# VectorE: addresses and wait values ahead of the drains, and a step's group sums ahead of the strong add of the expert before

## The reference, cut to what matters

```python
for l in range(L):                                   # L = 3
    agg = jax.ops.segment_sum(h[src], dst, num_segments=N) / deg
    logits = jnp.concatenate([h, agg], axis=-1) @ router_W[l] + router_b[l]
    vals, idx = jax.lax.top_k(logits, TOPK)
    gates = jax.nn.softmax(vals, axis=-1)
    gate_dense = jnp.zeros_like(logits).at[rows, idx].set(gates)
    weak = jax.nn.relu(jnp.einsum('nh,ehf->nef', agg, weak_W[l]) + weak_b[l])
    sh = jax.nn.relu(jnp.einsum('nh,ehf->nef', agg, strong_W1[l]) + strong_b1[l])
    strong = jnp.einsum('nef,efh->neh', sh, strong_W2[l]) + strong_b2[l]
    moe = jnp.einsum('ne,neh->nh', gate_dense, jnp.concatenate([weak, strong], axis=1))
    conf = jax.nn.sigmoid(h @ conf_W[l] + conf_b[l])
    h = h + conf * moe
```

## Time and profile before

| What | us |
|---|---|
| Median of 3 runs | 8162.51 |
| The profiled execution | 8152.95 |
| Its span in the profile | 8151.3 |
| Preparation, to the first transposes of means | 567 |
| Expert loops of layers 0, 1, 2, last two steps included | 1461, 1468, 1413 |

### The profile page before, as it was taken

One profiled execution on the slowest core, in us unless ns is written; L12 is line 12 of the kernel. 1 busy time (PEld: TensorE's weight loads), 2 busy tenths in 40 slices (PEclk: granted clock), 3 DMA queues, 4 the chain that ended last, 5 costly groups with the idle time before them and its releaser, 6 DMA issues.

```text
span 8151.3 us, 58255 instructions
## 1 busy us (share of the span) xinstructions
PE 3661.2 (45%) x12045; PEld 2192.1 (27%) x12045; DVE 3263.1 (40%) x6294; ACT 1297.7 (16%) x2725; POOL 4118.8 (51%) x4324
## 2 busy tenths in 40 slices
PE   3137777776577777674866757760000000000000
PEld 2124444443444433344433434450000000000000
DVE  2124444443243433333433333433445444454553
ACT  0002222222122212221222222221000000000000
POOL 5664445444454444444444353426556565665565
PEclk6558888887688888786887878875555555555555
DMA  2342222222322222223212121212122122111111
GB/s 67 86 113 70 66 70 76 73 73 69 85 74 64 65 72 67 72 71 90 61 56 67 54 70 54 58 32 49 44 48 47 45 48 41 45 46 44 41 45 42
DMA packets 259372, 500.85 MB, mean 61 GB/s; under 512 B 104429, under 2 KB 146344, under 8 KB 258878
## 3 DMA queue, kind: packets, MB, share of 16 engines
q0 software_dynamic: 176592, 446.04, 21.0%
q1 hardware_dynamic: 62718, 36.97, 1.7%
q10 hardware_dynamic: 19952, 16.60, 0.6%
HBM read 464.44 MB, written 34.88 MB: 61 GB/s over the span
## 4 chain that ended last, share of the span: by engine, by line
PE 34%; issue 24%; another core or an unknown queue 16%; DVEq 12%; DVE 8%; ACT 2%; POOL 2%; ACTq 1%; DMA 0%; SPq 0%; POOLq 0%
PE ps_w1a L1949 6%; PE ps_w1b L1949 6%; PE ps_gate L1974 5%; PE ps_wide L1974 4%; PE ps_weak_a L1961 3%; PE ps_weak_b L1961 3%; DVE ps_wide L1395 2%; DVEq L1427 2%; DVEq L1367 1%; DVEq L1440 1%; PE ps_weak_a L1933 1%; POOL ring L660 1%; DVEq L1437 1%; DVEq L1420 1%
## 5 line engine op out<-in xcount | busy, mean ns | idle before, releaser
L660 POOL DMA_INDIRECT ring<-hidden_tab,stage x2400 | 2290.5, 954 | 2632.1 <-DVE ps_wide L974 1675.1
L660 POOL DMA_INDIRECT ring<-gat_tab,stage x1600 | 1527.7, 955 | 1186.1 <-issue 664.8
L1949 PE MATMUL ps_w1a<-agg_team_t,wbuf 128*128 128x512 f32 (+1 forms) x1248 | 661.9, 649 | 324.3 <-issue 163.6
L1949 PE MATMUL ps_w1b<-agg_team_t,wbuf 128*128 128x512 f32 (+1 forms) x1248 | 626.1, 627 | 127.4 <-ACT strong L1603 81.0
L1974 PE MATMUL ps_gate<-wbuf,strong 128*128 128x256 f32 x2400 | 607.2, 394 | 108.0 <-issue 107.3
L980 DVE TENSOR_TENSOR ps_wide<-ps_wide,ring 128x1024 f32<-128x1024 f32 x418 | 515.7, 1234 | 229.8 <-issue 229.6
L1147 DVE TENSOR_TENSOR h_res<-h_res,x_res 128x1024 f32 (+2 forms) x117 | 136.2, 1164 | 1104.5 <-ACT x_res L1612 1059.4
L1974 PE MATMUL ps_wide<-wbuf,strong 128*128 128x256 f32 x2304 | 571.7, 397 | 0.9 <-issue 0.9
L2088 PE MATMUL ps_w1a<-ident,agg_team_t 128*128 128x128 f32 x28 | 7.8, 434 | 1255.8 <-DVE agg_team_t L1473 1114.5
L1974 PEld LDWEIGHTS ps_gate<-wbuf,strong 128*128 128x128 f32 x2400 | 448.8, 197 | 245.2 <-issue 180.9
L1974 PEld LDWEIGHTS ps_wide<-wbuf,strong 128*128 128x128 f32 x2304 | 440.3, 202 | 89.7 <-issue 7.4
(11 more groups left out here) (406 smaller groups left out, 4725.0 us busy)
## 6 DMA issues: line engine op xcount, KB each, us to landing
ring<-hidden_tab,stage POOLq DMA_INDIRECT x2400
ring<-gat_tab,stage POOLq DMA_INDIRECT x1600
hidden_tab<-h_res ACTq DMA_DIRECT2D x24, 512.0 KB, 3.0
hidden_tab<-h_res SPq DMA_DIRECT2D x12, 512.0 KB
wbuf<-in_L_gnn_strong_W SPq DMA_DIRECT2D x6, 1024.0 KB
wbuf<-in_L_gnn_strong_W SPq DMA_DIRECT2D x12, 512.0 KB
gat_tab<-h_res SPq DMA_DIRECT2D x12, 272.0 KB
wbuf<-in_L_gnn_weak_W SPq DMA_DIRECT2D x6, 512.0 KB
```

Of the source, the lines that this page charges most:

```text
L660: return pool.indirect_dma_start(out=ring[:, b, 0:width], out_offset=None, in_=table, in_offset=bass.IndirectOffsetOnAxis(ap=stage[:, half ...
L1949: last = mm(ps_w1[c % 2][:, 0:size * P], w1_w[:, k, s, c * P:(c + 1) * P], agg_team_t[:, k, 0:size * P], start=k == 0, stop=k == 1)
```

## The change

`address` lowers operands and `compute_val` a wait value, so that their registers are worked out at that place of the program; the instruction behind uses what was worked out. In `sum_units` this now comes before the drain, and the boundary of the group's end is loaded behind the first sum instead of ahead of it. In layer 0 the copy of the places stands before the drain and behind the wait. The drain behind the four last parts becomes one inside `mean_of`. In the loops the strong and weak adds work out address and wait value ahead of their drains; in steps written out with a constant number they stay as they were. In `step` the group sums move ahead of the strong add, and two drains go. Cut to its core:

```diff
+            def address(*operands):
+                for a in operands:
+                    dve.lower_ap(a)
+
-            def sum_units(r, first, last, begun, ended):
+            def sum_units(r, first, load_last, begun, ended):
+                def settle(r, u, count):
+                    if r == 0:
+                        dve.wait_ge(arrived, count)
+                        note_places(r, u)
+                        dve.drain()
+                    else:
+                        dve.compute_val(count)
+                        dve.drain()
+                        dve.wait_ge(arrived, count)
...
-                dve.drain()
-                dve.wait_ge(arrived, first + 1)
-                note_places(r, first)
-                nc.vector.scalar_tensor_tensor(wide_s, begun..., 0.5, rows(first), ALU.is_lt, ALU.mult)\
-                    .then_inc(ring_free, 1)
-                with dve.Fori(first + 1, last) as u:
-                    dve.drain()
-                    dve.wait_ge(arrived, u + 1)
-                    note_places(r, u)
-                    nc.vector.tensor_tensor(wide_s, wide_s, rows(u), ALU.add).then_inc(ring_free, 1)
+                begins, landed = begun.unsqueeze(2).to_broadcast([P, SLOTS, H]), rows(first)
+                address(landed, begins)
+                settle(r, first, first + 1)
+                nc.vector.scalar_tensor_tensor(wide_s, begins, 0.5, landed, ALU.is_lt, ALU.mult).then_inc(ring_free, 1)
+                last = load_last()
+                with dve.Fori(first + 2, last + 1) as after:
+                    u = after - 1
+                    landed = rows(u)
+                    address(landed)
+                    settle(r, u, after)
+                    nc.vector.tensor_tensor(wide_s, wide_s, landed, ALU.add).then_inc(ring_free, 1)
+                parts = [(slot(last, b), ended(b)) for b in range(SLOTS)]
+                for landed, ends in parts:
+                    address(landed, ends)
+                dve.compute_val(last + 1)
                 dve.drain()
                 dve.wait_ge(arrived, last + 1)
-                for b in range(SLOTS):
-                    nc.vector.scalar_tensor_tensor(wide_s[:, b, :], slot(last, b), ended(b), wide_s[:, b, :], ALU.mult, ALU.add)
-                dve.drain()
+                for b, (landed, ends) in enumerate(parts):
+                    nc.vector.scalar_tensor_tensor(wide_s[:, b, :], landed, ends, wide_s[:, b, :], ALU.mult, ALU.add)
...
             def mean_of(g, n, j):
...
+                address(own, on, scale)
+                dve.drain()
...
             def add_strong(r, q, s, size):
...
+                if isinstance(q, int):
+                    dve.drain()
+                    dve.wait_ge(mo_copied, n * 2 * NS + (2 * s + 2))
+                else:
+                    address(hq)
+                    dve.compute_val(n * 2 * NS + (2 * s + 2))
+                    dve.drain()
+                    dve.wait_ge(mo_copied, n * 2 * NS + (2 * s + 2))
...
                     for s in range(1, NS):
+                        at = gather_next(s, at)
                         between()
                         add_strong(r, q, s - 1, size)
-                        dve.drain()
-                        at = gather_next(s, at)
                         between()
                         if s < size:
-                            dve.drain()
                             add_weak(r, q, s, size, scratch)
```

More of the change, by code:

```diff
@@ L990, in mean_of @@
             def mean_of(g, n, j):
-                nc.vector.scalar_tensor_tensor(wide[:, 0:H], h_res[:, bass.ds(g, 1), :].rearrange("p a n -> p (a n)"), self_on[:, bass.ds(g, 1)],
-                                               wide[:, 0:H], ALU.mult, ALU.add)
+                own, on, scale = h_res[:, bass.ds(g, 1), :].rearrange("p a n -> p (a n)"), self_on[:, bass.ds(g, 1)], rdeg[:, bass.ds(g, 1)]
+                address(own, on, scale)
+                dve.drain()
+                nc.vector.scalar_tensor_tensor(wide[:, 0:H], own, on, wide[:, 0:H], ALU.mult, ALU.add)
                 dve.drain()
@@ L998, in mean_of, with load_last @@
                     w(dve, tr_ready, n * 2)
-                return nc.vector.tensor_scalar(agg4[:, j, :], part[:], rdeg[:, bass.ds(g, 1)], None, ALU.mult)
+                return nc.vector.tensor_scalar(agg4[:, j, :], part[:], scale, None, ALU.mult)
             def aggregate(r, q, j, c0=None):
                 g, n = q * TEAM + j, q + r * BATCHES
+                ends_at = []
+                def load_last():
+                    ends_at.append(dve.value_load(unit_at[0:1, bass.ds(g + 1, 1)], min_val=1, max_val=SMAX))
+                    return base + ends_at[0]
                 if c0 is None:
                     c0 = dve.value_load(unit_at[0:1, bass.ds(g, 1)], min_val=0, max_val=SMAX)
-                c1 = dve.value_load(unit_at[0:1, bass.ds(g + 1, 1)], min_val=1, max_val=SMAX)
                 base = units_before(r) + (apart * LEAD if r else 0)
-                sum_units(r, base + c0, base + c1, before_cut[:, bass.ds(g, 1), :].rearrange("p a s -> p (a s)"),
+                sum_units(r, base + c0, load_last, before_cut[:, bass.ds(g, 1), :].rearrange("p a s -> p (a s)"),
                           lambda b: before_cut[:, bass.ds(g + 1, 1), b:b + 1].rearrange("p a s -> p (a s)"))
-                return mean_of(g, n, j), c1
+                return mean_of(g, n, j), ends_at[0]
             def units_before(r):
@@ L1018, in part_units @@
                 c0 = dve.value_load(part_unit[0:1, i:i + 1], min_val=0, max_val=SMAX)
-                c1 = dve.value_load(part_unit[0:1, i + 1:i + 2], min_val=1, max_val=SMAX)
-                sum_units(r, units_before(r) + c0, units_before(r) + c1, part_before[:, i, :], lambda b: part_before[:, i + 1, b:b + 1])
+                sum_units(r, units_before(r) + c0, lambda: units_before(r) + dve.value_load(part_unit[0:1, i + 1:i + 2], min_val=1, max_val=SMAX),
+                          part_before[:, i, :], lambda b: part_before[:, i + 1, b:b + 1])
+                dve.drain()
             def early_units(r, first, last):
@@ L1143, in add_strong @@
                 n = q + r * BATCHES
-                dve.drain()
-                dve.wait_ge(mo_copied, n * 2 * NS + (2 * s + 2))
                 hq = team_of(q, size)
+                if isinstance(q, int):
[4 more added lines that the diff above has]
+                    dve.compute_val(n * 2 * NS + (2 * s + 2))
+                    dve.drain()
+                    dve.wait_ge(mo_copied, n * 2 * NS + (2 * s + 2))
                 last = nc.vector.tensor_tensor(hq, hq, scaled[s][:, 0:size, :], ALU.add).then_inc(mo_added, 1)
@@ L1153, in add_weak @@
                 n = q + r * BATCHES
-                dve.drain()
-                dve.wait_ge(weak_copied, n * 8 + (2 * j + 2 if size == TEAM else 8))
+                hg = h_res[:, bass.ds(q * TEAM + j, 1), :].rearrange("p a n -> p (a n)")
+                if isinstance(q, int):
+                    dve.drain()
+                    dve.wait_ge(weak_copied, n * 8 + (2 * j + 2 if size == TEAM else 8))
+                else:
+                    address(hg)
+                    dve.compute_val(n * 8 + (2 * j + 2 if size == TEAM else 8))
+                    dve.drain()
+                    dve.wait_ge(weak_copied, n * 8 + (2 * j + 2 if size == TEAM else 8))
                 nc.vector.tensor_reduce(o, weak_terms[j % 2], AX.X, ALU.add)\
```

2 lines of the change are left out of this document (removed).

## The result

The changed kernel takes 8230.69 us (median of 4 runs, 8225.56 to 8274.69), the kernel before beside it 8158.35: ratio 1.0105, 95% interval 1.0061 to 1.0149. The forecast was 7962, a gain. It was wrong in sign.

What follows compares the result with a forecast made beforehand. The prediction took TensorE, with 27% idle time in the expert loops, to bound the kernel. Its terms, 152 + 21 + 18 + 0 = 191 us off 8152.95, gave 7962 us, with a range of 7865 to 8115.

Steps and rivals of the forecast that it cites:

- the one on the ring: GpSimd's gathers in the expert loops: ring slots come free 12 to 20 us earlier, priced at nothing.
- The wait at L1923: TensorE's wait for the group means at the transposes opening a step goes: 152 us in layers 0 and 1.
- The seam: Between two steps: back branches cost some 20 us; VectorE's earlier branch saves 21 us, plus 18 in layer 2.
- Addresses ahead of the drains: VectorE's group sums: register work hidden saves 191 us on VectorE, 0 to 16 on TensorE's path, taken as 0.
- First rival, ScalarE's branch: At the seam, ScalarE's own back branch sets the pace; only seams without one gain, 49 us: 8104 us, 25%.
- Slower: Top of VectorE's loop grows by 22 instructions, 15 us a seam; 5 us net over 23 seams: 8268 us, 7%.
- What would show it: Signs if right: no wait at L1923, layer 1 steps of 115 to 119 us, gaps of 0.2 us before unit sums.

Runs made afterwards that it cites:

- e3: The changed kernel, but only group 3's sums stand ahead of the strong add, those of groups 1 and 2 behind theirs: 7915.72 us, ratio 0.9735.
- e2: The changed kernel with the old order (sums behind the strong add), addresses and wait values still ahead of the drains: 8002.08 us, ratio 0.9827.
- e18: The changed kernel, but group 2's sums alone stand behind their strong add, where engines crawl: 7904.82 us, ratio 0.964.
- e4: The changed kernel with ScalarE's step loops written out, so no back branch on ScalarE: 8217.66 us, ratio 1.0106.
- e9: The kernel before, with GpSimd waiting behind every sixteenth gather until those sixteen have landed: 7351.08 us, ratio 0.9024.
- e10: The changed kernel, with GpSimd waiting behind every sixteenth gather until those sixteen have landed: 7257.36 us, ratio 0.8931.
- e13: The changed kernel, but group 2's sums alone stand behind their strong add, where nothing crawls: 5796.33 us, ratio 0.9913.
- fourth set: Four follow-up runs sharing runs of the kernel before, which takes 5848.99 us there; their ratios run from 0.9913 to 1.1457.

## Why the prediction was wrong

The step that failed is the one on the ring, among the things that move: "Ring slots come free 12 to 20 us earlier, so GpSimd gathers earlier: with 2400 gathers in 2290 us and some 64 to a step of 126 it has slack, and I price this at nothing." The slack is real, and it is what lets the bursts join. GpSimd needs 5 us for the four gathers of a unit and VectorE frees a unit every 1.4 to 1.8, so a group's sums start a burst of 20 to 25 us. With group 2's sums some 18 us earlier (1009.66, 69 us behind the transposes at 940.4, for 1005.33, 88 behind 917.7), they free units before the burst of group 1 has ended: 36 gathers on end, through the last 28 us of which the other engines crawl. That is what the runs showed in place of "nothing": 451 us more of late time, against 364 us less outside it.

- *The wait at L1923 goes, 152 us.* Right, 2 us are left. By itself it is worth having, it seems: e3 is 86 us under e2 with the addresses alike (7915.72 to 8002.08), where e2's transposes still wait 106 us in layers 0 and 1. But e3 also moves the bursts off the seams, and the two were not separated.
- *The seam.* I laid its 20 us to back branches, and took the loop's end, where there are none, for proof. Wrong: in e3 and e18 the seams of the loops in layers 1 and 2 take 11.5 to 11.6 us, as at the loop's end, with all branches in place (layer 0: 11.5 to 16.7 behind its first), and e4 without ScalarE's is no faster. In the kernel before a burst opens with group 3's sums, from 3034.0 to 3068.7 in the step I read, so that most of the seam, from 3049 to 3072.7, lies in its late part; at the loop's end it opens at 3561.0 and the logits at 3567.57 are 7 us into it. Two explanations fitted the rows, and I had looked at the one only. The register moves of up to 716 ns in the earlier trace rows fit one slot of the crawling.
- *Addresses ahead of the drains, nothing.* Wrong by 126 us: e2's stretches sum to 4216 us, 4342 before. I had counted VectorE's gaps of 0.35 us and not that in a crawl its instructions cost 0.70 each. Its late time is as long as before (1443 us for 1442), but TensorE is busy for 41% of it instead of 35%. Which share is that, and which the wait at the transposes (152 to 106 us), was not separated.
- *First rival, ScalarE's branch.* Its picture came, with its cause refuted by e4: ScalarE stands longer since it crawls longer.
- *Slower.* The sign, but not the mechanism: the top of VectorE's loop in layer 1, from its back branch to the group's last sum, takes 6 to 7 us and took 17 to 30, and the kernel has 56886 instructions for 58255.
- *What would show it.* No wait at the transposes came, and unit gaps even of 0.09 us (the median in layer 1, for 0.35); layer 1's steps did not shrink to 115 to 119 us: seven of the nine between 2513 and 3644 us take 122 to 133.

With bursts capped at sixteen (e9, e10) the change gains 94 us, the sign and about half the size of the forecast, though by the order or the addresses is open. Where nothing crawls the nearest run, e13, gains 53 us.

What stays open: why a set crawls or not, and whether it would without the recording; what the engines share with GpSimd's gathers in a crawl (TensorE's, VectorE's and ScalarE's instructions come late, and no data transfer does: in the burst of 36 the last packet of a gather ends 2.4 us behind its start, early and late alike); why a few long bursts, as the one from 3561.0 to 3598.2 in the kernel before, show no crawl; whether the changed kernel itself gains where nothing crawls, as only e13 ran there; and group 1's move alone.

## What to carry to other kernels

Ask of every engine "off the path" not only whether it has slack but what its work does to the others while it runs, and whether a change joins its pieces; count its waits (105 against 73), not its busy time. When a stretch is slow with no releaser, line it up against all other engines before giving it a cause: here the line to GpSimd was in the first trace. And a tuning that pays by breaking such a pattern (13% here) must be timed again at other times and on other chips, and without the profiler: where nothing crawls, the same break costs 10%. The order with group 2's sums left in place, the one version besides the kernel before that ran in both conditions, gained in both, 3.6% and 0.9%.

## What the runs showed of the hardware

- In the first result and in four of the five sets of runs behind it, some 15 us into an unbroken run of indirect gathers (12 to 13 of them at 1.25 us) TensorE, VectorE and SyncE issue at multiples of 0.70 us (SyncE's two DMA issues at 1038.75 and 1042.26 in the changed kernel lie 3.51 apart), and ScalarE stands for up to 32 us, until 3 to 5 us after the run ends. A gap of 2.6 us behind each eight gathers keeps that away, one of 1.3 us only in part (ratios of 0.866 and 0.91).
- In the fourth set runs of 64 gathers and far more disturb nothing. The same kernel before takes 5849 us there and 8128 to 8201 in the others, 39 to 40% more, and one of those has the same chip number.
- Of the sixteen updates that each gather gives its semaphore, the traces hold all where nothing crawls, and 2.4 to 3.2 where it does and no break stands.
- TensorE's granted clock in layer 1 is 0.98 where it is fed without stops, 0.90 with breaks, 0.82 in the changed kernel.
